# Cross attention 0: three jobs taken from VectorE, and the value projection put in another tile of the turn

## The reference, cut to what matters

```
qw = (layer_norm(x) @ Wq + bq);  kw = (ctx @ Wk + bk);  vw = (ctx @ Wv + bv)      # 16 heads of 64 each
a  = einsum('bmhd,bnhd->bhmn', qw, kw) / sqrt(64)
a  = where(key_mask, a, -inf);  a = softmax(a)
o  = einsum('bhmn,bnhd->bmhd', a, vw);  x = x + o @ Wo + bo
```

## Time and profile before

| | us |
|---|---|
| median of 3 runs | 5843.41 (5843.09 to 5851.81) |
| profiled execution | 5850.3, its span 5848.6 |
| second pass of the cross attention (first to last scores) | about 372 to 2486 |
| from there to the start of the next part | to 2515 |

### The profile page before, as it was taken

How to read it: one execution, slowest core, us unless ns; L and a number is a source line. 1 busy time by engine, 2 the same in 40 slices (tenths; PEclk the granted TensorE clock), 3 DMA queues, 4 the chain that set the end, 5 groups by cost and what they waited for, 6 DMA issues and landing times. The chain is left out here.

```text
span 5848.6 us, 67075 instructions
## 1 busy us (share of the span) xinstructions
PE 5177.2 (89%) x26382; PEld 1639.8 (28%) x26382; DVE 3345.3 (57%) x3672; ACT 3414.0 (58%) x3486; POOL 2222.6 (38%) x1111
## 2 busy tenths in 40 slices
PE   8879999999999998879898689999886788888889
PEld 3223333333333333332343311111342111111123
DVE  5687878787878784315531400000257998888713
ACT  4566565665656566621122399999124677777761
POOL 1139898988989898905533000000000000000000
PEclk8889999999999999989999799999896799999999
DMA  1000000000000000010000220000203000000010
GB/s 50 15 1 1 1 1 1 1 1 1 1 1 1 1 1 1 1 42 1 2 1 6 71 64 17 13 12 2 80 26 125 12 11 11 11 12 12 7 46 31
DMA packets 64427, 100.61 MB, mean 17 GB/s; under 512 B 9846, under 2 KB 49880, under 8 KB 62000
## 3 DMA queue, kind: packets, MB, share of 16 engines
q1 hardware_dynamic: 63906, 95.50, 4.9%
q10 hardware_dynamic: 206, 0.83, 0.0%
HBM read 70.85 MB, written 25.31 MB: 16 GB/s over the span
## 5 line engine op out<-in xcount | busy, mean ns | idle before, releaser
L2494 ACT ACTIVATE Pr<-ps,key_bias 128x1024 f32<-128x1024 f32 x816 | 868.9, 1110 | 769.1 <-PE ps L2367 768.6
L2582 DVE TENSOR_REDUCE red<-ps 128x2 f32<-128x1024 f32 (+1 forms) x767 | 902.0, 1178 | 369.8 <-PE ps L2354 369.8
L2673 POOL TENSOR_TENSOR Ps<-Ps,Pr 128x1024 f32<-128x1024 f32 x400 | 946.7, 2367 | 214.1 <-ACT Pr L2494 212.9
L2682 POOL TENSOR_TENSOR Ps<-Ps,Pr 128x1024 f32<-128x1024 f32 x400 | 946.0, 2365 | 11.2 <-ACT Pr L2494 11.2
L3300 DVE TENSOR_REDUCE red<-ps 128x1 f32<-128x512 f32 (+3 forms) x1024 | 877.7, 908 | 95.6 <-PE ps L3173 76.2
L3256 ACT ACTIVATE Pr<-ps 128x1024 f32<-128x1024 f32 x816 | 786.2, 1021 | 230.3 <-PE ps L3183 229.4
L2367 PE MATMUL ps<-Q,Kr 64*128 64x512 f32 x3264 | 809.4, 610 | 58.0 <-DVE ps L2331 37.5
L2387 PE MATMUL ps<-Pr,Vc 128*64 128x512 f32 x3264 | 794.1, 607 | 0.0
L2331 DVE CAST ps<-seeds 128x1024 f32<-128x1024 bf16 x541 | 648.5, 1221 | 167.4 <-ACT Pr L2494 157.0
L3430 ACT ACTIVATE Pr<-ps 128x2048 f32<-128x2048 f32 x467 | 726.2, 2034 | 1.6 <-PE ps L3393 1.6
L3173 PE MATMUL ps<-Kp,Q 52*128 52x512 bf16 (+1 forms) x1664 | 442.6, 412 | 171.0 <-DVE red L3300 125.1
(11 more groups left out here) (574 smaller groups left out, 5152.5 us busy)
## 6 DMA issues: line engine op xcount, KB each, us to landing
L_dram_K<-parts SPq DMA_DIRECT2D x26, 384.0 KB, 2.9
Kp<-L_dram_K SPq DMA_DIRECT2D x14, 624.0 KB
L_dram_K<-parts SPq DMA_DIRECT2D x26, 256.0 KB, 2.9
wB<-L_ffn_shares SPq DMA_DIRECT2D x1, 6144.0 KB
w<-L_ffn_experts_w_dram SPq DMA_DIRECT2D x24, 256.0 KB
Kp<-L_dram_K SPq DMA_DIRECT2D x14, 416.0 KB
wB<-L_ffn_shares SPq DMA_DIRECT2D x1, 3584.0 KB, 12.8
ctx<-ctx_dram SPq DMA_DIRECT2D x13, 256.0 KB, 7.5
```

What stands on the lines that cost most here:

```text
L2494: nc.scalar.activation(Pr[:, t % 4, half].rearrange("p a n -> p (a n)"), ps[:, 2 * half:2 * half + 2, :].rearrange("p a n -> p (a n)"), AC ...
L2582: nc.vector.tensor_reduce(red[:, i // C % 2, q, :, i % C], ps[:, b:b + 2, 0:ctx.keys_in(i % C)], AX, ALU.max).then_inc(*reduced.up())
L2673: nc.gpsimd.tensor_tensor(into, into, src, ALU.add).then_inc(*summed0.up())
L2682: nc.gpsimd.tensor_tensor(into, into, src, ALU.add).then_inc(*summed1.up())
```

## The change

Seven edits, all in `cross_0`:

1. `spread_of_pair` and `mz` go. `neg` becomes bf16, and `rows` reads one column of it, repeated 128 times by its access pattern, as matmul weights.
2. The reciprocals of the first seven pairs are computed on a tile of 128x16: SP stores two rows of `over` in DRAM, loads them spread over 128 partitions, DVE inverts (`inverse_by_token`, turn LAG+C+1, step 3, which is c1), SP stores the result and loads it back, repeated over 64 partitions, into `over`. The last pair keeps its eight reciprocals.
3. The multiplication moves from c4, step 2, to c3, step 1, and the output from c5, step 1, to c4, step 1.
4. Bias and scale of the queries move from DVE to ACT, with a bias scaled in advance.
5. The values of the next chunk are projected in step 2 instead of step 0, behind the second maxima unit, and ACT copies them there.
6. In step 2 the second maxima unit now also goes to banks 0 and 1 (`s in (0, 2)`); with three units in a step 2, the middle one goes between the halves of the scores.
7. Seeds: DVE now has one half a tile, half 0 behind a `behind` unit and half 1 otherwise; ACT has the other half.

```diff
-    red, neg = k.tile(stack, "red", [128, 2, 8, 2, C]), k.tile(stack, "neg", [128, 8, 2])
-    mz = k.tile(stack, "mz", [128, 8, 2, 128], BF16)
+    red, neg = k.tile(stack, "red", [128, 2, 8, 2, C]), k.tile(stack, "neg", [128, 8, 2], BF16)
+    out_bias, bq_scaled = k.tile(stack, "out_bias", [128, 1]), k.tile(stack, "bq_scaled", [128, P])
+    sums_by_token = k.tile(stack, "sums_by_token", [128, S // 64])
+    sums_dram = [k.nc.dram_tensor(f"cross_0_dram_{n}", (2, S), F32, kind="Internal").ap() for n in ("sums", "inverse")]
+    turned = sums_dram[0].rearrange("a (p n) -> (a p) n", n=S // 64), sums_dram[1].rearrange("a (p n) -> (a p) n", n=S // 64)
...
-        return 0 if unit == items[-1] and len(items) > 1 and (s == 0 or others_at(g, s) or len(items) > 2) else 4
+        return 0 if unit == items[-1] and len(items) > 1 and (s in (0, 2) or others_at(g, s) or len(items) > 2) else 4
...
-    dve_seeds = [(t, half) for t in range(P * KT) for half in range(2) if half == 1 or t == 0 or behind(*tile_turns[t - 1])]
-    act_seeds = [(t, 0) for t in range(P * KT) if (t, 0) not in dve_seeds]
+    dve_seeds = [(t, half) for t in range(P * KT) for half in range(2) if t == 0 or half == (0 if behind(*tile_turns[t - 1]) else 1)]
+    act_seeds = [(t, half) for t in range(P * KT) for half in range(2) if (t, half) not in dve_seeds]
...
-        def keys(i, j):
-            if i < LAG:
-                take_banks(6, key_copied.at(i + 1))
-                if 0 <= j < N:
-                    take_banks(4, value_set.at(j + 1))
-            else:
-                take_banks(4, *([key_copied.at(i + 1)] if i < N else []), *([value_set.at(j + 1)] if 0 <= j < N else []))
+        def keys(i):
             if i < N:
+                take_banks(key_bank(i), key_copied.at(i + 1))
                 p, c = i // C, i % C
                 nc.tensor.matmul(ps[:, key_bank(i), :], lhsT=wk[:, p * 128:(p + 1) * 128], rhs=masked[:, c * CHUNK:(c + 1) * CHUNK], start=True, stop=True).then_inc(*key_mm.up())
 
         def values(j):
             if 0 <= j < N:
+                take_banks(4, value_set.at(j + 1))
...
-                    mm = nc.tensor.matmul(ps[:, 4 + a, q * 128:(q + 1) * 128], lhsT=mz[:, 4 * half + q, a, :], rhs=k.consts.ident16[:], start=True, stop=True)
+                    mm = nc.tensor.matmul(ps[:, 4 + a, q * 128:(q + 1) * 128], lhsT=neg[:, 4 * half + q, a:a + 1].to_broadcast([128, 128]), rhs=k.consts.ident16[:], start=True, stop=True)
...
-                if s == 0 or others or g < LAG:
+                if s in (0, 2) or others or g < LAG:
                     for q in between:
                         maxima(g, s, steps, q)
                 if 0 <= j < N:
                     scores(j, s, 1)
                 if s == 0:
-                    keys(g + 1, j + 1)
-                elif not others and g >= LAG:
+                    keys(g + 1)
+                elif s != 2 and not others and g >= LAG:
...
-                if s == 0:
+                if s == 2:
                     values(j + 1)
...
+                p = query_pair(g, s)
+                if p is not None:
+                    nc.scalar.wait_ge(*query_mm.at(p + 1))
+                    nc.scalar.wait_ge(*bias_scaled.at(1))
+                    if p >= 3:
+                        nc.scalar.wait_ge(*scored.at(2 * KT * (p - 2)))
+                        nc.scalar.wait_ge(*query_copied.at(p - 2))
+                    nc.scalar.activation(Q[:, p % 3, :], pair, ACT.Identity, bias=bq_scaled[:, p:p + 1], scale=scale).then_inc(*query_set.up())
...
                     nc.scalar.copy(over[:], pair).then_inc(*sums_set.up())
+                if s == 2 and 0 <= j + 1 < N:
...
+                for half in range(2):
+                    if 0 <= j < N and (t + 1, half) in act_seeds:
+                        seed(nc.scalar, nc.scalar.copy, t + 1, half, seeded_by_act)
...
+        def inverse_by_token(p):
+            nc.vector.wait_ge(*sums_in.dmas(p + 1))
+            nc.vector.reciprocal(sums_by_token[:], sums_by_token[:]).then_inc(*inverted.up())
...
-        def spread_of_pair(p):
-            nc.vector.wait_ge(*rows_step.at(2 * p + 1))
-            if p:
-                nc.vector.wait_ge(*rows_mm.at(2 * p))
-            nc.vector.tensor_copy(mz[:].rearrange("p q a n -> p (q a) n"), neg[:].rearrange("p q a -> p (q a)").unsqueeze(2).to_broadcast([128, 16, 128])).then_inc(*rows_step.up())
...
+                p = pair_for(g, s, LAG + C + 1, 3)
+                if p is not None and p < P - 1:
+                    inverse_by_token(p)
                 for n in range(8):
-                    p = weighted_pair(g, s, LAG + C + (2 * n + 2) // 4, (2 * n + 2) % 4, LAG + C + (n + 2) // 4, (n + 2) % 4)
-                    if p is not None:
-                        inverse(p, n)
-                p = weighted_pair(g, s, LAG + C + 4, 2, LAG + C + 2, 1)
+                    if pair_for(g, s, LAG + C + (n + 2) // 4, (n + 2) % 4) == P - 1:
+                        inverse(n)
+                p = weighted_pair(g, s, LAG + C + 3, 1, LAG + C + 2, 1)
                 if p is not None:
-                    nc.vector.wait_ge(*inverse_step.at(9 * p + 8))
+                    if p < P - 1:
+                        nc.vector.wait_ge(*over_in.dmas(2 * p + 2))
+                    else:
+                        nc.vector.wait_ge(*inverse_step.at(p + 8))
                     nc.vector.wait_ge(*acc_copied.at(p + 1))
                     nc.vector.tensor_tensor(Ur[:], Ur[:], over[:], ALU.mult).then_inc(*inverse_step.up())
...
+    def sp():
+        for p in range(P - 1):
+            nc.sync.wait_ge(*sums_set.at(p + 1))
+            for a in range(2):
+                nc.sync.dma_start(sums_dram[0][a:a + 1], over[64 * a:64 * a + 1, :]).then_inc(*sums_stored.dma())
+            nc.sync.wait_ge(*sums_stored.dmas(2 * p + 2))
+            if p:
+                nc.sync.wait_ge(*inverse_stored.dmas(p))
+            nc.sync.dma_start(sums_by_token[:], turned[0]).then_inc(*sums_in.dma())
+            nc.sync.wait_ge(*inverted.at(p + 1))
+            if p:
+                nc.sync.wait_ge(*over_in.dmas(2 * p))
+            nc.sync.dma_start(turned[1], sums_by_token[:]).then_inc(*inverse_stored.dma())
+            nc.sync.wait_ge(*inverse_stored.dmas(p + 1))
+            for a in range(2):
+                nc.sync.dma_start(over[head(a), :], sums_dram[1][a].unsqueeze(0).to_broadcast([64, S])).then_inc(*over_in.dma())
```

More of the change, by code:

```diff
@@ L2285, in others_at @@
         return [(item, p) for item, p in (("queries", query_pair(g, s)), ("first_rows", pair_for(g, s, C, 1)), ("second_rows", pair_for(g, s, C, 2)),
-                ("sums", pair_for(g, s, LAG + C, 1)), ("output", weighted_pair(g, s, LAG + C + 5, 1, LAG + C + 2, 2))) if p is not None]
+                ("sums", pair_for(g, s, LAG + C, 1)), ("output", weighted_pair(g, s, LAG + C + 4, 1, LAG + C + 2, 2))) if p is not None]
     def maxima_bank(g, s, steps, unit):
@@ L2433, in output @@
             take_banks(4, x_added.at(p + 1))
-            nc.tensor.wait_ge(*inverse_step.at(9 * p + 9))
+            nc.tensor.wait_ge(*inverse_step.at(p + 1 if p < P - 1 else p + 9))
             for half, sl in enumerate(HALVES):
@@ L2518, in act @@
                     nc.scalar.activation(Kb[:, i % 2, :], ps[:, key_bank(i), :], ACT.Identity, bias=bk[:, i // C:i // C + 1]).then_inc(*key_copied.up())
-                if s == 0 and 0 <= j + 1 < N:
-                    n = 128 * ctx.tiles_in((j + 1) % C)
-                    nc.scalar.wait_ge(*value_mm.at(j + 2))
-                    if j + 1 >= 3:
-                        nc.scalar.wait_ge(*weighed.at(KT * ((j - 2) // C) + min(KT, TPC * ((j - 2) % C + 1))))
-                    nc.scalar.copy(Vc[:, (j + 1) % 3, 0:n], ps[:, 5, 0:n]).then_inc(*value_set.up())
                 p = pair_for(g, s, LAG + C, 0)
@@ L2541, in act @@
                     if p:
-                        nc.scalar.wait_ge(*inverse_step.at(9 * p))
+                        nc.scalar.wait_ge(*inverse_step.at(p))
                     nc.scalar.copy(over[:], pair).then_inc(*sums_set.up())
+                if s == 2 and 0 <= j + 1 < N:
+                    n = 128 * ctx.tiles_in((j + 1) % C)
+                    nc.scalar.wait_ge(*value_mm.at(j + 2))
+                    if j + 1 >= 3:
+                        nc.scalar.wait_ge(*weighed.at(KT * ((j - 2) // C) + min(KT, TPC * ((j - 2) % C + 1))))
+                    nc.scalar.copy(Vc[:, (j + 1) % 3, 0:n], ps[:, 5, 0:n]).then_inc(*value_set.up())
                 t = KT * (j // C) + TPC * (j % C) + s
-                if 0 <= j < N and (t + 1, 0) in act_seeds:
-                    seed(nc.scalar, nc.scalar.copy, t + 1, 0, seeded_by_act)
+                for half in range(2):
+                    if 0 <= j < N and (t + 1, half) in act_seeds:
+                        seed(nc.scalar, nc.scalar.copy, t + 1, half, seeded_by_act)
     def dve():
@@ L2630, in dve @@
                                     nc.vector.wait_ge(*taken_off(g, q))
```

(4 more changed lines are left out.)

25 lines of the change are left out of this document (8 added, 17 removed).

## The result

The kernel after takes 5867.56 us (median of 6 runs, 5863.93 to 5867.98), the kernel before beside it 5847.85 (6 runs). The ratio is 1.0031, 95% interval 1.0018 to 1.0044: slower by about 18 us (the medians are 19.7 apart). The profiled execution took 5867.85 us, span 5866.1.

What follows compares the result with a forecast made beforehand. PE bounds regular turns, so time is won only where PE waits for DVE. Middle pairs at +2.7 each, +15 in all, first pair +8, pair 6 0, pair 7 -1, copy -1: +21 on 5843.4 gives 5864 us, range 5810 to 5905.

Steps and rivals of the forecast that it cites:

- The wait behind step 0: Before the next tile's first scores, PE waits for DVE's reduction and seed of half 0: 0.56 us a regular turn.
- The wait in step 2: Second maxima unit, now in banks 0 and 1, awaits the exponential of half 0: 0.55 us a regular turn.
- The stretch before it: Ahead of the cross attention's second pass, a copy of 1.2 us goes: -1 us.
- c3: Turn of a middle pair: +0.15, and the moved multiplication delays the reduction freeing bank 4 by about 0.45: +0.6 us.
- c0: Turn of a middle pair: step 0 loses values and waiting, ACT's seed of half 1 comes late: -0.2 us in all.
- The wait behind `rows`: In c12, step 2, the values wait until ACT has copied `rows` out of bank 4: 1.6 us.
- The first pair: Second pass's first pair, without reciprocals: ten turns lose 1.11 us each, c10 to c12 give 3.2 back: +8 us.
- The pair without a clock drop before: One of five middle pairs has no clock drop behind the copy to `mz` today and so gains 1.6 us less.
- (1): Rival: new waits in the regular turns are absorbed; both gives 5771 us (chance 0.10), only one 5817 (chance 0.14).
- (2): Rival: at its new place the multiplication waits for POOL to run dry, 6 pairs x 7 us: 5906; chance 0.12.
- (3): Rival: inverses come late, DMAs of 10 us instead of 3; near 5880, chance 0.05 together with more clock drops.
- (4): Rival: the change does less than it says, rows and multiplications cost the same; near 5843 us, chance 0.04.

Runs made afterwards that it cites:

- experiment 10: Kernel after with the keys of step 0 issued behind that step's second maxima unit: 5852.64 us, ratio 0.9996 to the kernel before.
- experiment 1: Kernel after with edits 5 and 6 undone: 5781.45 us, ratio 0.9884 to the kernel before.
- experiment 2: Kernel before with edits 5, 6 and 7 alone: 5901.66 us, ratio 1.0093 to the kernel before.
- experiment 9: Kernel after with a spare 128x512 reduction on DVE ahead of the multiplication of pairs 0 to 6: 5893.4 us, ratio 1.007 to the kernel before.
- experiment 3: Kernel after with step 2's values ahead of its second maxima unit instead of behind it: 5898.25 us, ratio 1.0082 to the kernel before.
- experiment 4: Kernel after with half of the values ahead of step 2's second maxima unit and half behind: 5863.89 us, ratio 1.0022 to the kernel before.
- experiment 8: Kernel before with edits 2 and 3 alone: 5822.81 us, ratio 0.9951 to the kernel before.
- experiment 11: Kernel before with edit 4 alone: 5847.15 us, ratio 0.999 to the kernel before.
- experiment 5: Kernel after with edits 5, 6 and 7 undone, leaving edits 1 to 4: 5784.4 us, ratio 0.9882 to the kernel before.
- experiment 7: Kernel before with edit 1 alone: 5820.81 us, ratio 0.9945 to the kernel before.
- experiment 12: Kernel after with edits 5 and 6 undone, and edit 7 kept except behind step 0 of c0: 5774.37 us, ratio 0.9862 to the kernel before.

## Why the prediction was right

**The two waits: right in kind and in sum, each a little off in size.** The wait behind step 0 was put at 0.56 and measures 4.79 - 4.12 = 0.67 (experiment 10 removes exactly this). The wait in step 2 was put at 0.55 and costs 0.41 (in experiment 10 step 0 grows by 5.93 - 5.52 when the keys no longer hide it). Step 2 by itself is longer by 5.88 - 4.26 - 1.09 = 0.53, as predicted, but step 3 then is 0.14 shorter (4.12 instead of 4.26), which the prediction did not have. The sum is 1.06 to 1.08 against 1.11. Experiment 1 shows that edits 5 and 6 are all of it. The row's idle time understates the first: 0.40 idle against 0.67 lost. The rest is in PE's busy time, 19.56 against 19.25 in the regular turn. In both places the idle time was less than the loss, and the distance between repeated rows was the price.

**The total: the mechanism was right, and some luck lies in the number.** The second pass was put at 15 + 8 + 0 - 1 = +22 and measures +16.5: the five middle pairs gave 10.4 instead of 15. The stretch before it, put at -1, came out at +2.8 and the one behind it at -1.8, neither of them explained. The forecast of 5864 also stands on a median before of 5843.4; the kernel before that ran beside the kernel after took 5847.85, and with it the same sum would have given 5869.

**The reliefs.** Edits 1, 2 with 3, and 4 give 4.16, 4.0 and 0.86 us a pair by themselves, 9.0 together, and 8.93 when they are made together (260.53 against 269.46): they add up, for each stands at another place. Edit 7 gives 0.93 more. Edits 5 and 6 take 11.6 (271.20 against 259.60). In the prediction this subtraction is hidden in sums by turn; it is the shorter account of the result. It depends on the order, though: added to the kernel before, edits 5 to 7 cost only 6.8 (276.23 against 269.46, experiment 2), and in that turn edits 1 to 4 give only 5.0 (276.23 against 271.20), since the new gaps already take in much of the work that they remove.

**Mis-sized terms.** Of the +2.7 a pair, 1.74 was measured. c3 was the largest error (+0.6 predicted, +0.17 measured): the multiplication delays the reduction, but PE's unit in step 2 waits for the exponential anyhow, so most of the 0.45 is covered. c0 gave 0.24 more than expected. Of the other turns each is within 0.15. The wait behind `rows` measures 1.39 against 1.6, the new reciprocal 0.24 against 0.15 without any effect (c1 is 20.31 like a regular turn). The first pair lost 8.1 (8), pair 6 lost 0.1 (0), pair 7 gained 2.1 (1). The pair without a clock drop before lost 3.35, 1.6 more than its neighbours, as the prediction had it.

**The rivals.** (1) fell: neither wait is absorbed, and experiment 1 is what its 5771 would have been (5781). (2) did not occur in the middle pairs, but its mechanism is real: in the kernel after the multiplication is 0.17 us early, as at its old place, and experiment 9 shows what a few tenths cost. The order of arrival was read too simply: the multiplication comes while a POOL operation is running in either case, 0.22 us before that one's end in the kernel after and 1.93 us before it in experiment 9, and each time it ends 1.1 us after that end (1259.75 + 1.30 against 1259.97, 1265.22 + 3.01 against 1267.15). The price of 7 us was too high for the middle pairs: 2.3 us where the clock holds, up to 5.3 with a lower clock behind the gap, since DVE gets in at the end of the running operation. In pair 7 it does not get in: there the multiplication lasts 12.7 us (13.5 before) and ends 1.1 us after the fifth POOL operation behind the running one. That is the run until POOL is dry that the prediction feared. POOL's operations follow one another without a gap in experiment 9 too, and what decides between the two cases no run here shows. The rule of the Trainium skill that was weighed there (SBUF — State Buffer, Who interferes with whom), exclusion for a whole instruction, agrees with the middle pairs in both orders: POOL stretched to 3.34 where it has to wait, DVE to 3.01 where it does. In pair 7 DVE is held for six instructions and not for one. An exclusion is also seen at the copy to `mz` before (2888 ns at the median, 1226 at least; POOL's operation that comes during it takes 3.11 instead of 2.36). (3) fell: the last transfer lands after 3.8 us, and nobody waits. (4) fell: every edit moves something, and the sum is small because two parts nearly cancel.

The busy share of DVE did not tell where a relief pays. Edit 4 moved one job to ACT in a turn where DVE is busy 17.57 of 22.96 us, and c10 fell by 0.86. Edit 7 took DVE from 15.15 to 14.13 of 19.25 in the regular turn of experiment 1, much the same share, and the turn stayed. The largest relief, edit 1, took away a copy that PE was waiting for (c12 down by 4.2). The rule of the Trainium skill on offloading (Perfetto Trace Analysis, Optimizing Scalar/DVE Operations) speaks of a saturated DVE; by the busy share none of these turns has one, so the rule does not tell them apart.

**What stays open.** Why the seed gap costs 0.27 beyond its idle time was not taken apart; the modelled ends of the matmuls don't resolve it. Why the values ahead of the unit (experiment 3) cost c3 and c0 so much was not tried. Edits 5 and 6 were never run apart from each other, nor without edit 7, so the split of their cost rests on experiments 3, 4 and 10. Why POOL holds DVE for one operation in experiment 9 and for six in pair 7 is not known.

## What to carry to other kernels

A change that bundles several edits can hide a large gain behind a large loss: 0.3% slower here was 1.2% of relief (experiment 1), and 1.5% of new cost, most of it in two waits. Where an accumulation bank is borrowed between two uses, as here, work must stand on both sides of the borrowed slot: ahead of it to cover the reader that frees the bank, behind it to cover the chain that hands it back. Before a job is moved out of such a place, measure how long it had been covering, and move only what nobody leans on.

## What the runs showed of the hardware

A two-input DVE operation on SBUF tiles and POOL's exclude each other: DVE's took 3.01 instead of 1.30 us where it had to wait for the end of one POOL operation, 12.7 where it waited for six (the running one and five more), and POOL's 3.34 instead of 2.36 where it had to wait for DVE's. DVE's reductions and seeds, which read or write PSUM, ran beside the same POOL operations without stretching either (1.22 and 2.36). After 2.48 us of idle time PE's granted clock was 0.63 of full over 4.57 us in one pair of the kernel before (most of that stretch at the 1.2 GHz level), and 1.00 (2.4 GHz) in the next pair at the same place, with the same 2.49 us of idle time:

```profile
1425.15:1429.72 4.57, 4.57 (x18) 2.30 (x16) 3.58 (x3) 1.63 (x3) 1.93 (x1) 0.63 0.00 0
1693.23:1697.57 4.34, 4.33 (x20) 1.85 (x21) 2.81 (x3) 1.85 (x3) 3.32 (x2) 1.00 0.00 2
```

That is part of the 1.6 us by which the pairs before differ (269.46 and 267.85), and such differences come and go in the pairs of experiments 8 and 11 too, which keep the copy to `mz`. In experiment 9 the gap of 2.31 us was followed by 1.00 in two pairs and by a lower clock in four (0.70 over 5.76 us in pair 3). In experiments 1, 5, 7 and 12, which do without that copy, the pairs 1 to 5 agree within 0.1 us.
